# Convolution stage of a gated block: products that span both heads, their sums through PSUM, statistics on ScalarE, three row buffers

## The chip, the cores and the metric

The kernel runs on one core of a Trainium2 chip. The metric is the device time of one execution in microseconds; lower is better. The kernel is written by hand against the engines: TensorE (PE), VectorE (DVE), ScalarE (ACT), GpSimd (POOL) and the DMA-issuing SyncE (SP) each run their own program in order and wait for each other through semaphores.

## The reference

```
x = x + tanh(g_xattn) * xattn(ctx, ctx, layernorm(x), ssm_kernel, D)
x = x + tanh(g_ffn)   * ffn(layernorm(x))

xattn: for batch b, head h (32), rows i, j of the head (8 x 8), length L = 512:
  kv[b,i,j,h,:] = k[b,h,i,:] * v[b,h,j,:]          (k = v = ctx)
  y   = causal convolution of kv with ssm_kernel[h], + D[h] * kv
  out[b,h,j,:] = sum over i of y[b,i,j,h,:] * q[b,h,i,:]
ffn: softmax gate over 16 experts, top 2 routed SwiGLU experts (512 -> 352 -> 512),
  plus two shared ones of the same size, on 2048 rows of 512
```

All of it is float32. Every large matrix is split into a high and a low part, and three products (high by high, high by low, low by high) make one matmul of full precision.

## The kernel before, in words

The first stage has 16 tiles, each of two heads, 8 rows per head and 8 batches: 128 rows of x. A tile's length of 512 is cut into four blocks of 128. Because k = v, only 36 of the 64 products kv of a head are formed (GpSimd, form; ScalarE, square), 288 columns with the batches. conv(t, lb) on TensorE multiplies them with Toeplitz matrices, for each of the two heads into its own PSUM bank (ps_conv[lb % 2] is a pair of banks): 6, 12, 18 and 24 matmuls for blocks 0 to 3. products(t, lb) on VectorE multiplies the result with q (the normalized x, transposed by turn_q and copied by q_copy). A head's 36 pairs give 5 rows of 64 columns that must be added. Three instructions per head do it, one into prod in SBUF and two into ps_rows in PSUM, and a seventh adds the two tiles of 512 into rows. sum_rows(t, lb) on TensorE transposes and adds the four parts of rows and the fifth of prod into a quarter of ps_o with five matmuls against the identity. residual(t) on VectorE then makes x2 out of ps_o, followed by its statistics (bn_stats, bn_aggr), and scale_x2, norm_x2, turn_t, tT_copy and gate make the normalized, transposed x2 and the expert logits.

The order is written out by hand in a function turn(t) for each engine, called for three tiles, then in a loop of two, then for three more (pairs). In tile t:

- TensorE: conv 0, sum_rows(t-1, 3), conv 1, gate(t-2), sum_rows(t, 0), conv 2, sum_rows(t, 1), conv 3, turn_t(t-1), turn_q(t+1), sum_rows(t, 2). conv(t, lb) waits for the products of block lb-2; sum_rows(t, 0) also for x2 of tile t-1, which frees ps_o.
- VectorE: products 0, residual(t-1) with statistics, logits_copy(t-2), products 1, scale_x2(t-1), scale_x(t+1), products 2, products 3.
- ScalarE: split_shared(t), split_kv_hi(t+1), std_x(t+1), std_x2(t-1), square(t+2), norm_x2(t-1), norm_x(t+1), q_copy(t+1), tT_copy(t-1).
- SP (line 467): load ctx(t+3), load x(t+2), store x2(t-1), load xr(t+1), load stage(t+2), store t(t-1), store tT(t-1), load the two Toeplitz parts(t+2). Each store waits for its data, and everything behind it waits too.

The second stage runs the experts: 16 tiles of rows with two shared experts, 47 slots of 128 routed rows. Its schedule is a list of units. Rows of a tile of shared work are loaded by SP (load_rows), rows of a routed tile gathered by GpSimd (gather), into tn[o % 2]; results leave by accumulating indirect DMAs (add_out), each of which waits for the one before it. In GpSimd's program of unit n, gather stands ahead of add_out. The routing itself (maxima, ranks, tables) is computed by VectorE in the first 15 units.

## Time and profile before

| what | value |
|---|---|
| time, median of 3 runs | 743.13 us (741.87 to 744.69) |
| profiled execution | 748.91 us, span 747.1 us |
| TensorE matmuls | 719.4 us busy, 96% of the span |
| TensorE weight loads | 677.7 us, 91% |
| VectorE | 568.9 us, 76% |
| ScalarE | 459.8 us, 62% |
| GpSimd | 369.6 us, 49% |
| mean granted TensorE clock | 0.995 of full speed |
| first stage | first convolution 11.0, last ends 208.1 us |

The matmuls of an engine are pipelined and their ends are modelled: a conv matmul is recorded with 0.30 us while the next one starts 0.13 later, so the distance of the starts says what one costs.

### The profile page before, as it was taken

The page shows a single profiled execution, that of the slowest core. Times are in us where ns is not written, and L with a number is a line of the kernel's source. Part 1 is how long each engine was busy: PE and PEld are TensorE (multiplying, and loading weights), DVE is VectorE, ACT ScalarE, POOL GpSimd, SP SyncE. Part 2 cuts the span into 40 slices and gives each one's busy share as a digit, 9 for nine tenths or more (in the row PEclk, how much of TensorE's full clock was granted, in tenths as well). Part 3 has the DMA queues.
Part 4 walks back from the last instruction along what each step waited for, and adds up shares of the span by engine and source line. Part 5 has one row for each costly group of instructions (what it writes and reads, how often), then busy time and mean ns, then how long its engine had stood idle before and what let it go on. Part 6 is the DMA issues. An engine that isn't in the chain of part 4 may idle for free.

```text
span 747.1 us, 15553 instructions
## 1 busy us (share of the span) xinstructions
PE 719.4 (96%) x4602; PEld 677.7 (91%) x4602; DVE 568.9 (76%) x1111; ACT 459.8 (62%) x659; POOL 369.6 (49%) x190
## 2 busy tenths in 40 slices
PE   3999999999999999999999999999989999999998
PEld 3999999999998999899988999888989999999997
DVE  7899989898955578428889588848977689679942
ACT  7575757566432322136978677747976699678941
POOL 4998888886400065032444444334634445434420
PEclk9999999999999999999999999999999999999999
DMA  7678787776522122463567577767655764332101
GB/s 240 221 231 274 222 265 231 256 235 231 171 100 43 29 43 43 141 184 97 164 201 209 124 234 214 178 174 167 159 159 168 170 194 88 73 67 51 29 16 56
DMA packets 48404, 114.88 MB, mean 154 GB/s; under 512 B 7472, under 2 KB 8624, under 8 KB 48336
## 3 DMA queue, kind: packets, MB, share of 16 engines
q1 hardware_dynamic: 35792, 89.67, 36.9%
q0 software_dynamic: 12544, 24.40, 17.3%
q8 instruction: 31, 0.51, 0.3%
q14 instruction: 37, 0.30, 0.1%
HBM read 157.78 MB, written 29.26 MB: 250 GB/s over the span
## 4 chain that ended last, share of the span: by engine, by line
PE 71%; DVE 11%; DMA 8%; issue 5%; ACT 3%; ACTq 1%; DVEq 0%; SPq 0%; POOLq 0%
PE pair L1304 20%; PE bank L1304 15%; PE pair L1329 12%; PE pair L1235 8%; PE bank L1329 7%; DMA out<-ys,slot_info 5%; PE bank L1186 4%; PE pair L1312 3%; PE bank L1246 2%; DVE prod L830 2%; DVE bank L835 2%; DVE x L801 2%; DVE rows L842 1%; DVE st L781 1%; DVE bank L838 1%
## 5 line engine op out<-in xcount | busy, mean ns | idle before, releaser
L1151 DVE TENSOR_TENSOR w_lo<-raw,w_hi 128x1408 fp32r<-128x1408 f32 x94 | 148.6, 1622 | 49.8 <-ACT w_hi L734 49.7
L1442 POOL DMA_INDIRECT out<-ys,slot_info x47 | 83.0, 1765 | 120.7 <-ACT ys L722 85.5
L1429 POOL DMA_INDIRECT tn<-t_rows,slot_info x47 | 77.2, 1643 | 119.6 <-DVE tT_lo L889 87.5
L734 ACT ACTIVATE w_hi<-raw 128x1408 fp32r x94 | 124.6, 1374 | 3.0 <-issue 2.5
L1235 PE MATMUL pair<-kv_hi,toep_hi 128*128 128x288 f32 x320 | 100.6, 314 | 2.0 <-DMA toep_lo<-kpad_lo 1.7
L1235 PE MATMUL pair<-kv_lo,toep_hi 128*128 128x288 f32 x320 | 95.3, 298 | 0.0
L1235 PE MATMUL pair<-kv_hi,toep_lo 128*128 128x288 f32 x320 | 95.2, 297 | 0.0
L1156 DVE TENSOR_TENSOR w_lo<-raw,w_hi 128x1536 fp32r<-128x1536 f32 x47 | 82.4, 1752 | 6.5 <-ACT w_hi L741 6.5
L1380 POOL TENSOR_TENSOR kv_lo<-kv,kv_hi 128x2304 fp32r<-128x2304 f32 x15 | 77.3, 5155 | 6.1 <-ACT kv_hi L626 6.1
L741 ACT ACTIVATE w_hi<-raw 128x1536 fp32r x47 | 69.2, 1473 | 1.5 <-DMA raw<-in_weights 1.1
L830 DVE TENSOR_TENSOR prod<-pair,q 128x256 f32<-128x256 f32 x128 | 53.5, 418 | 15.5 <-PE pair L1235 10.1
L1160 DVE TENSOR_TENSOR hid<-hid,pair 128x352 f32<-128x352 f32 x44 | 22.7, 517 | 55.4 <-ACT hid L748 55.4
L1235 PEld LDWEIGHTS pair<-kv_hi,toep_hi 128*128 128x128 f32 x320 | 61.0, 191 | 2.8 <-DMA toep_lo<-kpad_lo 2.3
L1235 PEld LDWEIGHTS pair<-kv_lo,toep_hi 128*128 128x128 f32 x320 | 61.2, 191 | 0.0
L1235 PEld LDWEIGHTS pair<-kv_hi,toep_lo 128*128 128x128 f32 x320 | 61.0, 191 | 0.0
L374 POOL TENSOR_TENSOR kv<-cx 128x1536 f32<-128x1536 f32 x15 | 52.6, 3506 | 13.9 <-DMA cx<-in_ctx 13.6
L748 ACT ACTIVATE hid<-pair 128x352 f32<-128x352 f32 x43 | 19.5, 454 | 59.3 <-PE pair L1304 59.2
L1442 POOL DMA_INDIRECT out<-ys,own_row x14 | 26.3, 1876 | 59.8 <-ACT ys L722 51.5
L1304 PE MATMUL pair<-w_hi,tT_hi 128*128 128x352 f32 x192 | 46.3, 322 | 2.6 <-DVE w_lo L1151 2.6
L1304 PE MATMUL pair<-w_hi,tT_lo 128*128 128x352 f32 x192 | 46.1, 321 | 0.0
L748 ACT ACTIVATE hid<-bank 128x352 f32<-128x352 f32 x36 | 16.3, 453 | 48.4 <-PE bank L1304 46.6
L1304 PE MATMUL pair<-w_lo,tT_hi 128*128 128x352 f32 x192 | 46.1, 321 | 0.0
(223 smaller groups left out, 2014.7 us busy)
## 6 DMA issues: line engine op xcount, KB each, us to landing
raw<-in_weights SPq DMA_DIRECT2D x94, 704.0 KB
raw<-in_weights SPq DMA_DIRECT2D x47, 768.0 KB
toep_hi<-kpad_hi SPq DMA_DIRECT2D x15, 512.0 KB, 4.5
toep_lo<-kpad_lo SPq DMA_DIRECT2D x15, 512.0 KB, 6.1
cx<-in_ctx SPq DMA_DIRECT2D x15, 384.0 KB, 6.3
stage<-in_weights SPq DMA_DIRECT2D x16, 272.0 KB, 6.6
xt<-in_x SPq DMA_DIRECT2D x16, 256.0 KB, 6.3
xr<-in_x SPq DMA_DIRECT2D x16, 256.0 KB, 6.5
```

The source lines that it names most:

```text
L374: eng.tensor_tensor(view(z, g0 * k + HB, [[k, g], [HB, 3], [1, HB]]), view(c, g0 * GW, [[GW, g], [0, 3], [1, HB]]), view(c, g0 * GW + BATC ...
L734: act.activation(w_hi[s % 2][:, a:b], raw[:, bass.ds(half + a, b - a)], ACT.Copy).then_inc(hi_ok[n_], 1)
L741: act.activation(w_hi[s % 2][:, W13:WROW], raw[:, bass.ds(half + W13, W2)], ACT.Copy).then_inc(hi_ok[2], 1)
L830: dve.tensor_tensor(view(pp, po, [[P + G, 4], [G, HD], [1, BATCH]]), view(y, 0, [[HB, 4], [BATCH, HD], [1, BATCH]]), view(qq, qo, [[0, 4], ...
L1151: dve.tensor_tensor(w_lo[s % 2][:, a:b], raw[:, bass.ds(half + a, b - a)], w_hi[s % 2][:, a:b].bitcast(F32), ALU.subtract).then_inc(lo_ok[ ...
L1156: dve.tensor_tensor(w_lo[s % 2][:, W13:WROW], raw[:, bass.ds(half + W13, W2)], w_hi[s % 2][:, W13:WROW].bitcast(F32), ALU.subtract).then_i ...
L1235: mm = pe.matmul(ps_conv[lb % 2][:, h * 512:h * 512 + n], w[p][:, k:k + P], z[p][:, o:o + n], start=(mb == 0 and m == 0), stop=(mb == lb a ...
L1304: mm = pe.matmul(dst[:, 0:INTER], a[:, c * P:(c + 1) * P], w[:, f:f + INTER], start=(c == 0 and k == 0), stop=(c == BLOCKS - 1 and k == 2))
L1329: mm = pe.matmul(y_bank(u.o)[:], a[:, c * P:(c + 1) * P], w[:, f0 + c * L:f0 + (c + 1) * L], start=(first and c == 0 and k == 0), stop=(la ...
L1380: pool.tensor_tensor(kv_lo[t.odd][:], kv[t.odd][:], kv_hi[t.odd][:].bitcast(F32), ALU.subtract).then_inc(kvl_ok, 1)
L1429: pool.indirect_dma_start(out=tn[o % 2][:], out_offset=None, in_=t_rows, in_offset=bass.IndirectOffsetOnAxis(ap=slot_info[:, 3 * i:3 * i + ...
L1442: pool.indirect_dma_start(out=out, out_offset=bass.IndirectOffsetOnAxis(ap=rows, axis=0), in_=ys[o % 2][:], in_offset=None, bounds_check=R ...
```

## The change

One products(t, lb) covers both heads with three multiplications: 384 elements into prod (pairs (i, i+1) to (i, i+3) times q of the one member), 128 into prod (pairs (i, i+4), both members), and 512 into ps_rows (pairs (i, i) to (i, i+3) times q of the other member). Three additions of 256 columns follow: in place in ps_rows, into half_sum, and of these two into rows. TensorE is left with three transposes per sum_rows: two of rows and one of prod. The rows of a tile are ordered head first. The statistics of x2 come from two passes with an accumulator on ScalarE, as those of x did already, and std_x(t+2) stands between norm_x and q_copy. In the second stage tn has three buffers, rows are loaded or gathered one tile earlier, and three row tiles are loaded before the last turn of SP. Renamings (o % 2 to o % 3 in the readers of tn, declarations) are left out.

```diff
 PRODROWS = 5
-PROD_STEPS = 6
+PROD_STEPS = 3
+SUMROWS = 2
 EXPERTS, INTER = 16, 352
...
-            u, out = unit(n), []
-            if n == 0:
-                out.append(2)
-            if u and u.last:
-                out.append(u.o + 3)
-            return [o for o in out if o < len(ORDER)]
+            def at(o):
+                return max(last_unit(o - 4), 15 if ORDER[o][0] else 0)
+
+            return [o for o in range(3, len(ORDER)) if at(o) == n]
...
                 routed, j = ORDER[o]
                 if not routed and o not in MID:
-                    wait(sp, tTl_ok, o - 1)
-                    sp.dma_start(tn[o % 2][:], tT_t[j]).then_inc(tn_in[o % 2], 16)
+                    wait(sp, tTl_ok, o - 2)
+                    sp.dma_start(tn[o % 3][:], tT_t[j]).then_inc(tn_in[o % 3], 16)
             sp.wait_ge(kv_ok, 2 * TILES)
             sp.wait_ge(xn_ok, TILES)
-            for p in (0, 1):
-                sp.wait_ge(tT_out[p], 16)
-            load_rows(0)
-            load_rows(1)
+            sp.wait_ge(tT_out[0], 32)
+            sp.wait_ge(tT_out[1], 16)
+            for o in range(3):
+                load_rows(o)
             turn(At(TILES - 1))
             for which in ("x2", "t", "tT"):
...
             act.activation(small[:, 3:4], small[:, 0:1], ACT.Sqrt)
+            def stats(src, mv, ok, t):
+
+                p = t.odd
+                act.activation(spent[:], src[p][:], ACT.Copy, scale=-1.0 / L, accum_out=mv[p][:, 0:1]).then_inc(ok, 1)
+                wait(act, ok, t * 2 + 1)
+                act.activation(spent[:], src[p][:], ACT.Square, bias=mv[p][:, 0:1],
+                               accum_out=mv[p][:, 1:2]).then_inc(ok, 1)
+                wait(act, ok, (t + 1) * 2)
+
             def std_x(t):
-
-                p = t.odd
-                wait(act, x_in[p], (t.half() + 1) * 16)
+                wait(act, x_in[t.odd], (t.half() + 1) * 16)
                 wait(act, rstd1, (t - 1) * 2)
-                act.activation(spent[:], xt[p][:], ACT.Copy, scale=-1.0 / L, accum_out=mv1[p][:, 0:1]).then_inc(stat1, 1)
-                wait(act, stat1, t * 2 + 1)
-                act.activation(spent[:], xt[p][:], ACT.Square, bias=mv1[p][:, 0:1],
-                               accum_out=mv1[p][:, 1:2]).then_inc(stat1, 1)
-                wait(act, stat1, (t + 1) * 2)
-                act.activation(sd1[p][:, 0:1], mv1[p][:, 1:2], ACT.Sqrt, bias=small[:, 0:1],
+                stats(xt, mv1, stat1, t)
+                act.activation(sd1[t.odd][:, 0:1], mv1[t.odd][:, 1:2], ACT.Sqrt, bias=small[:, 0:1],
                                scale=1.0 / L).then_inc(std1, 1)
             def std_x2(t):
-                wait(act, stat2, (t + 1) * 2)
-                act.activation(sd2[t.odd][:, 0:1], mv2[t.odd][:, 1:2], ACT.Sqrt, bias=small[:, 0:1]).then_inc(std2, 1)
+                wait(act, x2_ok, t + 1)
+                wait(act, rstd2, (t - 1) * 2)
+                stats(x2, mv2, stat2, t)
+                act.activation(sd2[t.odd][:, 0:1], mv2[t.odd][:, 1:2], ACT.Sqrt, bias=small[:, 0:1],
+                               scale=1.0 / L).then_inc(std2, 1)
             def norm_x(t):
...
                 wait(act, prod_ok, (t - 1) * 4 * PROD_STEPS)
                 wait(act, q_turned, t + 1)
-                src = ps_q[:].rearrange("p (l c) -> p l c", l=BLOCKS)
-                dst = q[p][:].rearrange("p (l c) -> p l c", l=BLOCKS)
-                act.activation(dst[:, :, 0:P], src, ACT.Copy).then_inc(q_ok, 1)
-                act.activation(dst[:, :, P:], src[:, :, 0:GROUPS * EXT - P], ACT.Copy).then_inc(q_ok, 1)
+                act.activation(view(q[p][:], 0, [[2 * GW, BLOCKS], [GW, 2], [1, HB]]),
+                               view(ps_q, 0, [[P, BLOCKS], [HB, 2], [1, HB]]), ACT.Copy).then_inc(q_ok, 1)
+                act.activation(view(q[p][:], HB, [[2 * GW, BLOCKS], [GW, 2], [1, HB // 2]]),
+                               view(ps_q, 0, [[P, BLOCKS], [HB, 2], [1, HB // 2]]), ACT.Copy).then_inc(q_ok, 1)
             def tT_copy(t):
...
                 if first:
                     std_x(t + 1)
+                if first:
                     split_kv_hi(t + 1)
                 split_shared(t)
                 if not first and not last:
                     split_kv_hi(t + 1)
-                    std_x(t + 1)
                 if not first:
                     std_x2(t - 1)
...
                 if not last:
                     norm_x(t + 1)
+                if not t.within(TILES - 2, TILES):
+                    std_x(t + 2)
+                if not last:
                     q_copy(t + 1)
                 if not first:
...
                 dve.scalar_tensor_tensor(x2[p][:], ps_o[:], small[:, 1:2], xr[p][:],
                                          ALU.mult, ALU.add).then_inc(x2_ok, 1)
-                wait(dve, x2_ok, t + 1)
-                stats(x2, st2, mv2, stat2, t)
             def scale_x2(t):
                 p = t.odd
                 wait(dve, std2, t + 1)
                 dve.reciprocal(sd2[p][:, 1:2], sd2[p][:, 0:1]).then_inc(rstd2, 1)
                 wait(dve, rstd2, t * 2 + 1)
-                dve.tensor_scalar(mv2[p][:, 2:3], mv2[p][:, 0:1], sd2[p][:, 1:2], -1.0,
-                                  ALU.mult, ALU.mult).then_inc(rstd2, 1)
+                dve.tensor_scalar(mv2[p][:, 2:3], mv2[p][:, 0:1], sd2[p][:, 1:2], None,
+                                  ALU.mult).then_inc(rstd2, 1)
             def products(t, lb):
                 par = lb % 2
-                G, HB = GROUPS, HD * BATCH
-                for h in range(2):
-                    y = ps_conv[par][:, h * 512:h * 512 + 512]
-                    qo = lb * GROUPS * EXT + h * BATCH
-                    po = h * BATCH
-                    qq, pp = q[t.odd][:], prod[par][:]
-                    if h == 0:
-                        wait(dve, summed, t * 4 + lb - 1)
-                        if lb == 0:
-                            wait(dve, q_ok, (t + 1) * 2)
-                    wait(dve, conv_ok, t * 8 + 2 * lb + h + 1)
-                    dve.tensor_tensor(view(pp, po, [[P + G, 4], [G, HD], [1, BATCH]]),
-                                      view(y, 0, [[HB, 4], [BATCH, HD], [1, BATCH]]),
-                                      view(qq, qo, [[0, 4], [G, HD], [1, BATCH]]), ALU.mult).then_inc(prod_ok, 1)
-                    if h == 0:
-                        wait(dve, rows_ok, t * 4 + lb)
-                    dve.tensor_tensor(view(ps_rows, po, [[P, 3], [G, HD], [1, BATCH]]),
-                                      view(y, HB, [[HB, 3], [BATCH, HD], [1, BATCH]]),
-                                      view(qq, qo + G, [[G, 3], [G, HD], [1, BATCH]]), ALU.mult).then_inc(prod_ok, 1)
-                    dve.tensor_tensor(view(ps_rows, po + 3 * P, [[4 * G, 2], [G, 4], [1, BATCH]]),
-                                      view(y, 4 * HB, [[0, 2], [BATCH, 4], [1, BATCH]]),
-                                      view(qq, qo + 4 * G, [[4 * G, 2], [G, 4], [1, BATCH]]), ALU.mult).then_inc(prod_ok, 1)
+                y, z, w = ps_conv[par][:], q[t.odd][:], prod[par][:]
+                qo, n = lb * 2 * GW, 4 * HB
+                wait(dve, summed, t * 4 + lb - 1)
+                if lb == 0:
+                    wait(dve, q_ok, (t + 1) * 2)
+                wait(dve, conv_ok, t * 8 + 2 * lb + 2)
+                dve.tensor_tensor(view(w, BATCH, [[n, 2], [HB + BATCH, 3], [1, HB]]),
+                                  view(y, HB, [[512, 2], [HB, 3], [1, HB]]),
+                                  view(z, qo, [[GW, 2], [0, 3], [1, HB]]), ALU.mult).then_inc(prod_ok, 1)
+                dve.tensor_tensor(view(w, 2 * n, [[HB, 2], [HB // 2, 2], [1, HB // 2]]),
+                                  view(y, 4 * HB, [[512, 2], [0, 2], [1, HB // 2]]),
+                                  view(z, qo + HB // 2, [[GW, 2], [HB // 2, 2], [1, HB // 2]]),
+                                  ALU.mult).then_inc(prod_ok, 1)
+                wait(dve, rows_ok, t * 4 + lb)
+                dve.tensor_tensor(view(ps_rows, 0, [[HB, 2], [P, 4], [1, HB]]),
+                                  view(y, 0, [[512, 2], [HB, 4], [1, HB]]),
+                                  view(z, qo, [[GW, 2], [BATCH, 4], [1, HB]]), ALU.mult).then_inc(prod_ok, 1)
                 wait(dve, prod_ok, (t * 4 + lb + 1) * PROD_STEPS)
-                dve.tensor_tensor(rows[par][:], ps_rows, prod[par][:, 0:L], ALU.add).then_inc(rows_ok, 1)
+                m = SUMROWS * P
+                dve.tensor_tensor(ps_rows[:, m:], ps_rows[:, m:], view(w, 2 * HB, [[HB, 2], [n, 2], [1, HB]]),
+                                  ALU.add).then_inc(half_ok, 1)
+                dve.tensor_tensor(half_sum[:], ps_rows[:, 0:m], view(w, 0, [[HB, 2], [n, 2], [1, HB]]),
+                                  ALU.add).then_inc(half_ok, 1)
+                wait(dve, half_ok, (t * 4 + lb + 1) * 2)
+                dve.tensor_tensor(rows[par][:], ps_rows[:, m:], half_sum[:], ALU.add).then_inc(rows_ok, 1)
             def first_kv_lo(a, b, ok):
...
                     wait(pe, x2_ok, t)
                 wait(pe, rows_ok, t * 4 + lb + 1)
-                for r in range(PRODROWS):
-                    part = (rows if r < BLOCKS else prod)[lb % 2]
-                    mm = pe.matmul(ps_o[:, lb * P:(lb + 1) * P], part[:, r * P:(r + 1) * P], ident[:],
-                                   is_transpose=True, start=(r == 0), stop=(r == PRODROWS - 1))
+                last = prod[lb % 2][:, 8 * HB:]
+                for r in range(SUMROWS + 1):
+                    part = rows[lb % 2][:, r * P:(r + 1) * P] if r < SUMROWS else last
+                    mm = pe.matmul(ps_o[:, lb * P:(lb + 1) * P], part, ident[:],
+                                   is_transpose=True, start=(r == 0), stop=(r == SUMROWS))
                 mm.then_inc(summed, 1)
...
                     pool.wait_ge(r_done, 1)
-                wait(pool, tTl_ok, o - 1)
-                pool.indirect_dma_start(out=tn[o % 2][:], out_offset=None, in_=t_rows,
+                wait(pool, tTl_ok, o - 2)
+                pool.indirect_dma_start(out=tn[o % 3][:], out_offset=None, in_=t_rows,
                                         in_offset=bass.IndirectOffsetOnAxis(ap=slot_info[:, 3 * i:3 * i + 1], axis=0),
-                                        bounds_check=ROWS - 1, oob_is_err=False).then_inc(row_in[o % 2], 16)
+                                        bounds_check=ROWS - 1, oob_is_err=False).then_inc(row_in[o % 3], 16)
...
-    x_rows = x.reshape(BATCH, TILES, 2, HD, L).transpose(1, 3, 2, 0, 4).reshape(ROWS, L)
+    x_rows = x.reshape(BATCH, TILES, 2, HD, L).transpose(1, 2, 3, 0, 4).reshape(ROWS, L)
```

## Rows read from the trace of the kernel before

**Rows 1.** Busy time by stretch, 13 tiles of the first stage: from, to, length, busy.
```profile
38.61:197.94 159.33, 157.58 (x1250) 154.52 (x1250) 144.45 (x481) 101.81 (x182) 134.11 (x50) 1.00 0.75 240
```
**Rows 2.** Instructions in order of time, VectorE, one tile: start, length, idle before.
```profile
97.91 0.42 DVE L830 TENSOR_TENSOR prod<-pair,q 128x256 f32<-128x256 f32 x1 [0.48 <-PE pair L1235]
...
99.86 0.42 DVE L830 TENSOR_TENSOR prod<-pair,q 128x256 f32<-128x256 f32 x1 [0.39 <-ACT q L612]
...
100.46 0.22 DVE L838 TENSOR_TENSOR bank<-pair,q 128x64 f32<-128x64 f32 x1
100.59 0.42 DVE L830 TENSOR_TENSOR prod<-pair,q 128x256 f32<-128x256 f32 x1
...
101.19 0.22 DVE L838 TENSOR_TENSOR bank<-pair,q 128x64 f32<-128x64 f32 x1
101.45 0.69 DVE L842 TENSOR_TENSOR rows<-bank,prod 128x512 f32<-128x512 f32 x1
102.05 0.74 DVE L801 SCALAR_TENSOR_TENSOR x<-bank,small,xr 128x512 f32<-128x512 f32 x1
...
103.91 0.42 DVE L830 TENSOR_TENSOR prod<-pair,q 128x256 f32<-128x256 f32 x1
...
106.74 0.41 DVE L830 TENSOR_TENSOR prod<-pair,q 128x256 f32<-128x256 f32 x1
```
**Rows 3.** The same view, TensorE, around the same tile.
```profile
97.58 0.30 PE L1235 MATMUL pair<-kv_hi,toep_lo 128*128 128x288 f32 x1
...
98.15 0.60 PE L1186 MATMUL bank<-ident,xn 128*128 128x128 f32 x4
...
103.92 0.29 PE L1235 MATMUL pair<-kv_hi,toep_hi 128*128 128x288 f32 x1
...
105.51 0.29 PE L1235 MATMUL pair<-kv_hi,toep_hi 128*128 128x288 f32 x1
...
106.25 0.66 PE L1246 MATMUL bank<-ident,rows 128*128 128x128 f32 x4 [0.18 <-DVE rows L842]
...
106.77 0.38 PE L1235 MATMUL pair<-kv_hi,toep_hi 128*128 128x288 f32 x1
```
**Rows 4.** The same view, ScalarE and SP's queue, the same tile.
```profile
98.85 0.60 ACT L611 ACTIVATE q<-bank 128x512 f32<-128x512 f32 x1 [3.03 <-PE bank L1186]
...
99.60 0.60 ACT L618 ACTIVATE tT<-bank 128x512 f32<-128x512 f32 x1
...
102.65 0.64 ACT L577 ACTIVATE spent<-xt 128x512 f32<-128x512 f32 x1
...
104.46 0.28 ACT L587 ACTIVATE sd<-mv,small 128x1 f32<-128x1 f32 x1
...
100.23 0.35 SPq L465 DMA_DIRECT2D tT_rows<-tT  x1
...
103.09 0.35 SPq L434 DMA_DIRECT2D xt<-in_x  x1
```
**Rows 5.** DMA issues, from 36 to 204 us and to 48 us: count, KB, landing.
```profile
xt<-in_x SPq DMA_DIRECT2D x12, 256.0 KB, 6.2
...
xt<-in_x SPq DMA_DIRECT2D x1, 256.0 KB, 8.0
```
**Rows 6.** Hand-over: order of time (TensorE, ScalarE), then the chain of waits.
```profile
228.52 0.59 PE L1304 MATMUL pair<-shared_hi,tT_hi 128*128 128x352 f32 x2 [1.81 <-DVE hid L1160]
...
222.72 0.63 ACT L707 ACTIVATE tT_hi<-tn 128x512 fp32r<-128x512 f32 x1 [2.30 <-DMA tn<-tT_rows]
...
228.52 5.68 PE pair L1304 x24
...
236.85 3.81 PE pair L1304 x24
```
**Rows 7.** Second stage: TensorE in order of time, then waits in total.
```profile
546.58 0.99 PE L1186 MATMUL bank<-ident,tn 128*128 128x128 f32 x4 [1.89 <-DMA tn<-t_rows,slot_info]
...
ACT ys L722 <- DMA out<-ys,slot_info: 34.4, 14, 6.4
```

More of the change, by code:

```diff
@@ L208, in program @@
         x2 = sb2("x2", [P, L], F32, one)
-        st2 = sb2("st2_", [P, 6], F32, one)
         mv1, mv2 = sb2("mv1_", [P, 3], F32, one), sb2("mv2_", [P, 3], F32, one)
@@ L217, in program @@
         prod = sb2("prod", [P, PRODROWS * P], F32, one)
-        rows = sb2("rows", [P, L], F32, one)
+        rows = sb2("rows", [P, SUMROWS * P], F32, one)
+        half_sum = sb("half_sum", [P, SUMROWS * P], F32, one)
         spent = sb("spent", [P, L], F32, one)
@@ L223, in program @@
         one.close()
-        tn = sb2("tn", [P, L])
+        tn = [sb(f"tn{n}", [P, L]) for n in range(3)]
         tn_mid = sb("tn_mid", [P, L])
@@ L290, in program @@
         r_fields, r_info, r_done = sem("r_fields"), sem("r_info"), sem("r_done")
-        tn_in, row_in, tn_mid_in = sem2("tn_in"), sem2("row_in"), sem("tn_mid_in")
+        tn_in, row_in = [sem(f"tn_in{n}") for n in range(3)], [sem(f"row_in{n}") for n in range(3)]
+        tn_mid_in = sem("tn_mid_in")
         tile_turned, tTh_ok, tTl_ok = sem("tile_turned"), sem("tTh_ok"), sem("tTl_ok")
@@ L355, in tn_count @@
         def tn_count(o):
-            return 16 * sum(ORDER[k][0] == ORDER[o][0] and k not in MID for k in range(o % 2, o + 1, 2))
+            return 16 * sum(ORDER[k][0] == ORDER[o][0] and k not in MID for k in range(o % 3, o + 1, 3))
         def last_unit(o):
@@ L776, in _ @@
             dve.tensor_tensor(krow_lo[:], krow[:], krow_hi[:].bitcast(F32), ALU.subtract).then_inc(krowl_ok, 1)
-            def stats(src, st, mv, ok, t):
-                p = t.odd
-                dve.bn_stats(st[p][:], src[p][:]).then_inc(ok, 1)
-                wait(dve, ok, t * 2 + 1)
-                dve.tensor_copy(hop[:, 1:2], hop[:, 0:1])
-                dve.bn_aggr(mv[p][:, 0:2], st[p][:]).then_inc(ok, 1)
             def scale_x(t):
@@ L1275, in turn_tile @@
             def turn_tile(o):
[L1276 removed]
+                pe.wait_ge(row_in[o % 3], tn_count(o))
                 wait(pe, tTl_ok, o)
[L1278 removed]
+                turn_rows(tn[o % 3], ps_t, tile_turned)
             def parts(hi, lo, whi, wlo):
```

15 lines of the change are left out of this document (7 added, 8 removed).

## The prediction

> **What bounds the kernel now.** I read the busy time by stretch first, then the instructions of one tile in order of time on each engine, then the DMA issues, and last the chain of waits after the first stage. In 159.3 us the first stage does 13 tiles, so a tile takes 12.26 us [rows 1]. TensorE is busy for 99% of them and VectorE for 91%, which looks like a TensorE that only needs less work. The order of time says otherwise: both engines stand in one loop and wait for each other once or twice per tile.
>
> The loop of today can be followed in the tile whose first product starts at 99.86 [rows 2]. VectorE does products of block 0 (to 102.05, so 2.19 us for a block), the residual, the statistics of x2, a logits copy and block 1, whose rows release TensorE's sum_rows at 106.25, after it sat idle [rows 3]. Then come 24 matmuls of block 3, 8 transposes, q_copy, and the next tile's first product, which had to wait for q_copy [rows 2, 4]. Check of the loop: 106.25 - 99.86 = 6.39; 0.60 for five transposes and the first conv's late start; 24 x 0.1325 = 3.18 (twelve conv matmuls take 105.51 - 103.92 = 1.59); turn_t 0.44; from turn_q's start to q_copy 0.70 and to the product 1.01 more [rows 3, 4]. Sum 12.32, against 12.26 measured. So I trust sums of this kind to 0.1 us.
>
> **The change, first stage.** Call the start of block 0's products zero.
>
> *Cost of products.* The old block has seven instructions over 1536 elements, the new one six over 1792 (384, 128, 512 multiplied; 256 + 256 + 256 added). A successor that waits for nothing starts 0.09 us before the record of its predecessor ends (100.46, 0.22 long, next at 100.59); one that waits for its result starts 0.04 after it (101.19, 0.22 long, next at 101.45) [rows 2]. An element costs (0.69 - 0.42)/256 = 1.05 ns. So: 384 elements 0.42 + 0.13 - 0.09 = 0.46; 128 elements 0.28 - 0.09 = 0.20; 512 elements with a wait behind it 0.69 + 0.04 = 0.73; add 0.33; add with a wait 0.46; add 0.33. Sum 2.51, so 0.32 more than 2.19. The pattern (runs of 64 in place of runs of 8) I price at nothing: the old ones already run at one element per 1.05 ns. No row shows an instruction that reads and writes the same PSUM bank, as the first add does. Bounds: 0 (it goes like the other mixes of PSUM and SBUF) to doubling, 0.27 per block; I take 0, the nearest rows, 0.42 for 256 elements out of PSUM.
>
> *The Trainium skill* ("VectorE: DVE Perf Modes", section "The DRAIN you can't avoid") says that the pipeline empties after every operation anyway and a semaphore wait costs nothing extra. The trace does not agree: the same 64-element product is followed after 0.13 us without a wait and after 0.26 with one [rows 2].
>
> *The new loop.* Block 0 ends at 2.51; the residual takes 0.74 and its result is seen 0.05 later: 3.30. Here TensorE waits in sum_rows(t, 0), because it may not write ps_o before x2 is out. Five transposes after a wait took 106.77 - 106.25 = 0.52 [rows 3]; three take 0.30, the first conv matmul's late start 0.08: 3.68. 18 conv matmuls: 2.39, 6.07. Three transposes: 0.33, 6.40. 24 conv matmuls: 3.18, 9.58. The products of block 3 now need both heads. Before, they did head 0 while TensorE computed head 1, and only head 1 was left at 97.91, 0.20 behind the end of the last conv matmul's slot (97.58 + 0.13) [rows 2, 3]. Now all of block 3 comes after it: start 9.78, end 12.29, and there the next tile's first product stands. Tile: **12.29 us**, 0.03 more than now. The 8 transposes less (0.88 us) and the statistics gone from VectorE (103.91 - 102.05 less 0.65 for the residual and some 0.12 for the logits copy, 1.09 us) are real, but they are given back: twice 0.32 for longer blocks, and the overlap lost at block 3, whose bare part grows from 1.46 us (0.73 for head 1, 0.13, 0.60) to 2.51. Fourteen tiles: +0.4.
>
> *What lies beside this loop.* q_copy: 9.58 + 0.44 + 0.70 + 1.01 = 11.73, 0.56 before it is needed [rows 4]. VectorE's own sum: 4 x 2.51 + 0.65 + 0.12 + 0.64 of scales (106.74 - 103.91 - 2.19) = 11.5. The statistics of x2 on ScalarE: the same pair of passes and the root for x take 104.46 - 102.65 = 1.81 [rows 4], from 3.3 to 5.2, and scale_x2 comes at 5.8; the cover is 0.6. ScalarE waited 3.03 us per tile before q_copy, and std_x(t + 2), moved there, takes 1.81 of it. But it must have x(t + 2), and that closes a second loop: tT_copy, SP's store of it, two toeplitz loads, ctx, the x load (issued 103.09 - 100.23 = 2.86 later), landing after 6.2 [rows 4, 5], statistics 1.81, 0.75 to tT_copy's start (99.60 - 98.85), 0.60 for it: 12.2 us and two hops. That ties with 12.29. In steady state I take nothing; one early tile has its x landing after 8.0 [rows 5], which costs (8.0 - 6.2 less slack of about 1.0) +0.8 once. The first tile, where block 3's products also lie bare, +0.3.
>
> **The change, hand-over and second stage.** The last block 3 ends 1.05 later behind its convolution and tT_lo(0) stands behind it; TensorE has its last gate and sums to do in the meantime, so I take +0.7 (bounds 0 and 1.05). Against this, row tile 2 of the expert stage is loaded before the last turn's stores, no longer behind them. ScalarE waited 2.30 us for it, and behind it stand tT_lo(2), the routing's first operations and the hidden rows of unit 2, for which TensorE sat idle 1.81 us. Its next 24 matmuls took 5.68 us where 3.81 is normal [rows 6]: after the idle the granted clock fell to its lower level (1.2 GHz) for part of them. The chain gets 2.3 us earlier while TensorE gets 0.7 later, so I take both: -1.8 and -1.9. Bounds: 0 to -4.2.
>
> Gathers of routed rows: fills_at moves each by one tile and the wait from o - 1 to o - 2, so at a given place of POOL's queue the same tT_lo is awaited; the add-outs behind it are not freed. What goes is TensorE's wait for a late gather, in the longest case 1.89 us and transposes of 0.99 instead of 0.60 [rows 7]. The larger waits here, ScalarE for earlier add-outs, 34.4 us in 14 times [rows 7], stay, and would swallow part of what an early gather gives. I take -1.2, bounds 0 to -6. SP's earlier row loads wait for results that are old by then: 0. More bytes move nowhere.
>
> **Sum.** First stage +0.4 + 0.8 + 0.3 = +1.5; hand-over +0.7 - 1.8 - 1.9 = -3.0; gathers -1.2; together **-2.7 us**. The profiled execution took 748.9 (span 747.1, 1.8 around it), so it would take 746.2; the runs' median, 743.1, lies 5.8 below the profiled one, and I move it by the same: **740.5 us**. I read "same" as within 0.5%, 3.7 us: 739.4 to 746.8.
>
> **Rivals.**
> - *The load of x decides (slower).* The second loop takes over once x lands more than about 0.1 to 0.3 us later than 6.2. For it: the tie, and landings of up to 8.0 [rows 5]. Against it: the transfers of one burst share a queue, so a later issue is likely to land sooner. At 0.5 us per tile: 14 x 0.5 = +7, 747.5. It decides from a tile of 12.55 us upward. Chance 0.20.
> - *The in-place add in one PSUM bank runs at half speed (slower).* Two blocks of the loop: 14 x 2 x 0.27 = +7.6, 748. Chance 0.08.
> - *Waits inside the products cost nothing (faster).* Each block would be 0.26 shorter, the loop 0.52, to 11.77; then the x loop (12.1) decides: -0.2 x 14 = -2.7, 737.8. For it stands only that TensorE and VectorE have less work each. Chance 0.12. This is also what the skill's rule above would make of it.
> - *The third buffer smooths the expert stage (faster).* If the stalls behind add-outs shrink too, with gathers landed early: 5 us more than I took, 735.5. Against it: they follow add-outs. Chance 0.15.
> - *Hand-over bound by another thing*, such as POOL's constants for the routing: nothing gained there but nothing lost, 744. Chance 0.06.
>
> Forecast 0.39; its own range 737.5 to 744. Faster by over 0.5%: the two fast rivals and 0.12 of the forecast's own, 0.39. Slower: the two slow ones less a little, 0.26. Within: 0.35. For eight in ten I take 735.5 to 748.5.
>
> **What would show it.** Products of 384, 128 and 512 elements of about 0.56, 0.28 and 0.69 us, adds of 0.42; 2.5 us per block; block 3's first product idle behind PE by about 0.8 us and the next tile's first product waiting for nothing; TensorE idle about 0.8 us before sum_rows(t - 1, 3) and 0.3 before sum_rows(t, 0). If that product waits for q_copy and ScalarE's first pass over x waits for its DMA, the second loop decides. If tiles take under 12.0, my cost of a block or of the bare block 3 is wrong. At the hand-over: no fall of the clock near 230 us. If it stays, the routing chain has another start than tile 2.

## The result: 6 us slower, and the profile after

| | median | range | runs |
|---|---|---|---|
| before | 743.13 us | 739.15 to 748.21 | 19 |
| changed | 749.71 us | 744.32 to 753.81 | 19 |

The ratio is 1.0082, 95% interval 1.0061 to 1.0104, so 6.1 us slower; on a second chip it was 1.0054 (1.0027 to 1.0082), 4.0 us. 740.5 was forecast, and the time lies outside the range. The profiled execution of the changed kernel took 747.88 us (span 746.0), that of the kernel before 748.91. So between the two executions whose traces are read here the changed kernel is 1.0 us faster, while over all runs it is 6.1 us slower: the traces show where single stages grew or shrank, and the runs decide the whole.

Busy time in the stretch of [rows 1], changed kernel (from, to, length; TensorE, its weight loads, VectorE, ScalarE, GpSimd, each with its count; granted clock, DMA share, GB/s):
```profile
38.61:197.94 159.33, 144.10 (x1116) 139.92 (x1115) 143.73 (x385) 122.08 (x228) 133.64 (x50) 1.00 0.75 238
```
TensorE fell from 99% to 90% busy and VectorE stayed at 90%: work was taken off, and the stage became longer. Where it went is seen in one tile of VectorE, in order of time (start, length, idle before), which answers to [rows 2]:
```profile
102.97 0.56 DVE L825 TENSOR_TENSOR prod<-pair,q 128x384 f32<-128x384 f32 x1 [0.26 <-issue]
103.44 0.28 DVE L828 TENSOR_TENSOR prod<-pair,q 128x128 f32<-128x128 f32 x1
103.64 0.69 DVE L833 TENSOR_TENSOR bank<-pair,q 128x512 f32<-128x512 f32 x1
104.36 0.43 DVE L838 TENSOR_TENSOR bank<-bank,prod 128x256 f32<-128x256 f32 x1
104.70 0.41 DVE L840 TENSOR_TENSOR half_sum<-bank,prod 128x256 f32<-128x256 f32 x1
105.15 0.43 DVE L843 TENSOR_TENSOR rows<-bank,half_sum 128x256 f32<-128x256 f32 x1
105.49 0.74 DVE L803 SCALAR_TENSOR_TENSOR x<-bank,small,xr 128x512 f32<-128x512 f32 x1
...
112.91 0.56 DVE L825 TENSOR_TENSOR prod<-pair,q 128x384 f32<-128x384 f32 x1 [0.93 <-PE pair L1236]
...
115.44 0.55 DVE L825 TENSOR_TENSOR prod<-pair,q 128x384 f32<-128x384 f32 x1
```
The same tile on TensorE (with the idle rows that answer to [rows 3]) and then on ScalarE [rows 4]:
```profile
102.76 0.44 PE L1248 MATMUL bank<-ident,rows 128*128 128x128 f32 x2 [0.71 <-DVE rows L843]
...
106.36 0.43 PE L1248 MATMUL bank<-ident,rows 128*128 128x128 f32 x2 [0.66 <-DVE x L803]
...
109.13 0.38 PE L1248 MATMUL bank<-ident,rows 128*128 128x128 f32 x2
...
112.64 0.60 PE L1187 MATMUL bank<-ident,t 128*128 128x128 f32 x4
```
```profile
111.41 0.63 ACT L576 ACTIVATE spent<-xt 128x512 f32<-128x512 f32 x1 [0.64 <-DMA xt<-in_x]
...
113.77 0.60 ACT L616 ACTIVATE q<-bank 128x512 f32<-128x512 f32 x1 [0.47 <-PE bank L1187]
```
The reader is to see the loop that was drawn: products of block 0, residual, sum of rows on TensorE, blocks 2 and 3 of the convolution, block 3's products bare behind them, and the next tile's product without a wait. From 102.97 to 115.44 it takes 12.47 us. At each of the four boundaries of VectorE's loop (two tiles per pass) VectorE idles 0.26 to 0.33 us more, put down to "issue" (the first line above is one of them), and the tile takes 12.74 to 12.82.

Starts of turn_q (L1187, the TensorE row that reads xn) in the two kernels, read from the same view:

| | tile 1 | tile 15 | a tile, mean of 14 | last conv matmul | expert stage starts | unit 3 | table's matmuls |
|---|---|---|---|---|---|---|---|
| before | 24.33 | 196.26 | 12.28 | 207.84 | 210.74 | 228.52 | 305.95 |
| changed | 24.83 | 200.71 | 12.56 | 212.53 | 216.28 | 232.41 | 308.23 |
| difference | +0.5 | +4.45 | +0.28 | +4.7 | +5.5 | +3.9 | +2.3 |

Unit 3 is the one whose up-projection (24 matmuls) TensorE waited 1.81 us for in the kernel before [rows 6]; the table's matmuls are the 32 that build the routing table.

The hand-over, chain of waits from 215 to 245 us, changed kernel, and the row in it of TensorE [rows 6]:
```profile
225.05 0.81 PE bank L1208 x8
225.98 0.08 issue
226.06 0.24 POOL io L1407
...
227.22 0.53 POOL upper L1418
227.74 0.06 issue
227.80 0.16 POOL own_row L1420
...
229.52 2.41 DVE mi L920 x17
231.93 0.43 DVE hid L1161
232.41 4.15 PE pair L1306 x24
```
```profile
232.41 0.59 PE L1306 MATMUL pair<-shared_hi,tT_hi 128*128 128x352 f32 x2 [0.17 <-DVE hid L1161]
```
The 1.81 us of idle and the 5.68 us are gone. What holds the routing's start is now the last gate (L1208) and GpSimd's constants behind it.

### The profile page after: what moved, and what is told of

The parts are those of the page before. It is cut to its first block, busy times and chain, and to the rows that moved or that the text cites. A ratio compares the mean times of both kernels' runs of the same rounds, so it can differ in the third digit from the quotient of the medians.

```text
span 746.0 us, 15248 instructions
## 1 busy us (share of the span) xinstructions
PE 706.5 (95%) x4474; PEld 664.1 (89%) x4474; DVE 571.2 (77%) x999; ACT 486.4 (65%) x723; POOL 366.6 (49%) x190
## 4 chain that ended last, share of the span: by engine, by line
PE 66%; DVE 12%; DMA 11%; issue 5%; ACT 2%; POOL 1%; DVEq 1%; ACTq 1%; SPq 0%; POOLq 0%
PE pair L1306 18%; PE pair L1236 13%; PE bank L1306 13%; PE pair L1331 11%; DMA out<-ys,slot_info 9%; PE bank L1331 6%; PE pair L1314 3%; DVE bank L833 2%; PE bank L1248 2%; PE bank L1187 2%; DVE bank L838 2%; DVE x L803 2%; DVE half_sum L840 1%; DVE prod L825 1%; DVE prod L828 1%
## 5 line engine op out<-in xcount | busy, mean ns | idle before, releaser
L1444 POOL DMA_INDIRECT out<-ys,slot_info x47 | 80.9, 1721 | 122.1 <-ACT ys L732 89.6
L825 DVE TENSOR_TENSOR prod<-pair,q 128x384 f32<-128x384 f32 x64 | 35.3, 552 | 16.6 <-PE pair L1236 15.4
```

The source lines that it names most:

```text
L825: dve.tensor_tensor(view(w, BATCH, [[n, 2], [HB + BATCH, 3], [1, HB]]), view(y, HB, [[512, 2], [HB, 3], [1, HB]]), view(z, qo, [[GW, 2], [ ...
L1444: pool.indirect_dma_start(out=out, out_offset=bass.IndirectOffsetOnAxis(ap=rows, axis=0), in_=ys[o % 2][:], in_offset=None, bounds_check=R ...
```

## The experiments

Each kernel was timed beside the kernel before on its chip. "Parts" are parts of the change alone, put on the kernel before.

**1. The third buffer alone.** Only the row buffers and semaphores by o % 3 and what goes with them:
```
+        tn = [sb(f"tn{n}", [P, L]) for n in range(3)]
-                    wait(sp, tTl_ok, o - 1)
+                    wait(sp, tTl_ok, o - 2)
```


> The kernel before with the third row buffer alone (tn[o % 3], gathers and row loads one tile earlier); the first stage is the one of before. All theories: last convolution ends at 208.1 us as before; the expert stage's up-projection of unit 3 starts 1.8 us earlier and without the slow stretch behind it, so unit 4 starts 3.5 us earlier than at 236.9. Theory A (the first stage alone makes the changed kernel slower, the third buffer only helps): total 3.5 us below before. Theory B (the third buffer costs some 4 us in the expert stage, as the medians suggest: both profiles stand 2.3 us apart at 350 us, the medians 6.6): total as before, within 1 us. Theory C (the new order of rows in a tile costs it): like A, 3.5 below, since this kernel keeps the old order.

Measured: 740.68 us, ratio 0.9961 (0.9938 to 0.9984), faster by 2.9; 3.5 was expected. In its trace, first in order of time and then in the chain of waits, the hand-over is that of the forecast:
```profile
227.18 0.59 PE L1303 MATMUL pair<-shared_hi,tT_hi 128*128 128x352 f32 x2 [0.30 <-DVE hid L1159]
```
```profile
227.18 4.14 PE pair L1303 x24
233.98 3.81 PE pair L1303 x24
```
Unit 4 begins at 233.98 and not at 236.85: 2.9 us, as large as the gain of the runs. 1.34 of it is the idle and 1.5 the fall of the clock (4.14 us for the 24 matmuls against 5.68). The runs of before hold that fall only as far as it is usual there; of the four kernels with two row buffers three have it in their profile (before and 2 with 5.68, 4 with 5.67), and 3 has not (4.14). On the first stage of before the third buffer does no harm in total.

**2. The first stage alone** (the changed kernel with two row buffers, the edit above undone).

> The changed kernel with two row buffers as before, so the first-stage change alone, with the new order of rows. All theories: tiles of 12.5 us on average, last convolution ends at 212.8, and the wait at the hand-over is back (unit 4 starts near 242). Theory A: 5.3 us above before, and the changed kernel would then be 3.5 us faster than this one, which its own median (6.6 above before) contradicts. Theory B: 5.3 above before, the changed kernel 1 us slower than this one. Theory C: 9 to 10 us above before.

Measured: 751.42 us, ratio 1.0094 (1.0064 to 1.0123), slower by 7.0. Its tiles are those of the changed kernel, 12.47 and 12.75 to 12.81, and unit 4 starts at 242.9: the wait at the hand-over is back. 1.0094 x 0.9961 = 1.0055: the two parts add up to the change within the intervals.

**3. The statistics alone**, on the kernel before: statistics of x2 on ScalarE and std_x moved; old products.
```
-                std_x(t + 2)          # before norm_x2
+                    std_x(t + 2)      # behind norm_x(t + 1)
+            def std_x2(t):
+                stats(x2, mv2, stat2, t)
```


> The kernel before with only the statistics of x2 on ScalarE (and std_x(t+2) between norm_x and q_copy). The loop of before loses 1.1 us on VectorE (11.2), so TensorE's own sum decides, 60 x 0.1325 + 28 x 0.11 + 0.9 = 11.9, with hops 12.0 a tile, if the x load's loop (12.1 to 12.3) allows it: 14 x -0.15 to -0.25, total 2 to 3.5 us below before. Rival: the x load's loop holds the tile at 12.26 or above: no gain, or a loss of up to 2 us.

Measured: 743.38 us, ratio 0.9995 (0.9976 to 1.0014). Its steady tiles take 12.1 us, which would gain about 2 us; but two tiles early in the stage took 12.95 and 15.45, where the first pass over x waited up to 4.0 us for its load. The waits from 36 to 66 us (engine, line, what for, total, times, longest):
```profile
ACT spent L574 <- DMA xt<-in_x: 9.5, 3, 4.0
DVE prod L828 <- PE pair L1233: 4.2, 7, 0.8
DVE prod L828 <- ACT q L617: 3.9, 2, 2.4
```
Here the second loop of the forecast is real: the load of x decides.

**4. The products alone**: new products, sums and three transposes; statistics still on VectorE.

> The kernel before with only the new products and sums (and the new order of rows), statistics of x2 still on VectorE. My loop over the residual and the bare block 3 gives 12.47 as in the changed kernel; VectorE's own sum is now 4 x 2.53 + 0.65 + 0.12 + 0.63 + 0.97 of statistics = 12.5, with the loop's branch in every second tile 12.7: 14 x 0.45, total 5 to 8 us above before. Rival (block 3's lost overlap is not on the path, the slow part lies elsewhere): tile of 12.26, total as before.

Measured: 762.46 us, ratio 1.0265 (1.023 to 1.0301), slower by 18 to 20. Its tile is 13.3 and 13.7 us, more than any theory had. VectorE, in order of time:
```profile
107.94 0.56 DVE L828 TENSOR_TENSOR prod<-pair,q 128x384 f32<-128x384 f32 x1 [0.28 <-issue]
...
110.47 0.74 DVE L804 SCALAR_TENSOR_TENSOR x<-bank,small,xr 128x512 f32<-128x512 f32 x1
111.24 0.69 DVE L784 BATCH_NORM_STATS2 st<-x 128x6 f32<-128x512 f32 x1
...
112.32 0.56 DVE L828 TENSOR_TENSOR prod<-pair,q 128x384 f32<-128x384 f32 x1
...
118.82 0.56 DVE L828 TENSOR_TENSOR prod<-pair,q 128x384 f32<-128x384 f32 x1 [0.73 <-PE pair L1239]
```
The loop passes over block 1 here: statistics lie between residual and block 1, whose rows TensorE needs before block 3 (112.32 + 2.6 = 114.9, then 0.4 of transposes, 3.18 of block 3, hop), and block 3's products stand bare behind that. So the products cost 18 us, and moving the statistics, worth nothing by itself, gives 11 of them back (762.46 against 751.42 in 2). Parts that lie in one loop do not add.

**5. The changed kernel again**, beside 6 to 8.

> The changed kernel itself, timed again beside the three that follow. At the first routing table's matmuls it stood 2.3 us behind the kernel before in the two profiles (308.2 against 305.9 us), while the medians differ by 6.1. Theory A (the difference is made in the first stage, and the profile of before is itself an unlucky one, 5.8 us above its median): the table at 308 to 309 us again and a time 5 to 7 us above before, about 749. Rival B (part of the 6.1 is made in the expert stage by the other row buffers or by the transfers that fall otherwise): the profile again at 308 us, but from there to the end some 3 us more than in the kernel with the third buffer alone (which needed 435.9 us from there to its end); A has 435 to 437 for that stretch.

Measured: 748.57 us, ratio 1.0054 (1.0027 to 1.0082); the profile (745.97) has the table's matmuls at 307.78 and 436.4 us from there to the end. This profile is as A has it, but it does not refute rival B. The same expert stage took 437.8 us in the first profile of the changed kernel, and 440.1 and 439.9 in those of 8 and 9. Over all the kernels' profiles that stretch is 434.4 (experiment 4) to 441.2 (the kernel before): the mean of the four with two row buffers is 437.6, that of the ten with three 438.9. B stays open, as a difference of 1 to 3 us that single profiles don't tell apart.

**6. TensorE's turn in another order**, on the changed kernel. Nothing is computed otherwise; conv gets a list of heads.
```
                 conv(t, 0)
+                conv(t, 1)
                 sum_rows(t - 1, 3)
-                conv(t, 1)
                 gate(t - 2)
+                conv(t, 2, (0,))
                 sum_rows(t, 0)
-                conv(t, 2)
+                conv(t, 2, (1,))
+                conv(t, 3, (0,))
                 sum_rows(t, 1)
-                conv(t, 3)
+                conv(t, 3, (1,))
```


> The changed kernel with TensorE's turn in another order: both blocks 0 and 1 before the sum of the last rows, and the sums of blocks 0 and 1 each put between the two heads of the convolution two blocks on. Theory A (a tile of the first stage is a closed chain VectorE block 3, VectorE block 0 and residual, TensorE sum of rows, convolutions 2 and 3, VectorE block 3; 12.47 us and 12.8 across the loop's branch): 0.66 us that TensorE waited for x2 and 0.7 for the rows before it are filled with convolution, so the tile falls to 11.7 to 12.1, 14 tiles give 7 to 12 us, and the time is 738 to 743. Rival C (the loop of the x load, xn done, load issued, x landed, statistics, xn, decides as soon as the other is shortened; 12.1 us a tile in the kernel with only the statistics moved): tile 12.1 to 12.3 with q_copy late and block 0 waiting for it, time 742 to 746. Rival D (VectorE's work itself binds, 4 x 2.52 + 0.8 + 0.5): tile 11.4 to 11.6 with no wait on VectorE, time 733 to 738.

Measured: 742.78 us, ratio 0.9968 (0.9942 to 0.9995), 5.8 under the changed kernel. The steady tiles are 11.8 to 12.1, as A and nearly C allow, and the idle before block 0's products and before the pass over x says C:
```profile
102.03 0.56 DVE L825 TENSOR_TENSOR prod<-pair,q 128x384 f32<-128x384 f32 x1 [0.57 <-ACT q L618]
...
114.11 0.56 DVE L825 TENSOR_TENSOR prod<-pair,q 128x384 f32<-128x384 f32 x1 [0.54 <-ACT q L618]
```
```profile
111.33 0.63 ACT L576 ACTIVATE spent<-xt 128x512 f32<-128x512 f32 x1 [1.50 <-DMA xt<-in_x]
```

**7. Block 3's products by head**, on the changed kernel.
```
-                wait(dve, conv_ok, t * 8 + 2 * lb + 2)
+                each = lb == 3
+                for h, k in ((0, 1), (1, 1)) if each else ((0, 2),):
+                    wait(dve, conv_ok, t * 8 + 2 * lb + h + k)
                     (the three products over k heads from head h)
```


> The changed kernel with block 3's three products made for each head apart, the first head's as soon as its convolution is done. Theory A (what decides is that VectorE now starts block 3 only when both heads are convolved, and does nothing in the 0.93 us before): products of head 0 (0.28 + 0.14 + 0.35 = 0.77 us) go into that wait, three instructions' fixed cost of about 0.1 each comes back, so block 3 ends about 0.6 us earlier and the tile is 11.9 to 12.0; 14 tiles give 8 us and the time is 740 to 743. Rival C (the x load's loop takes over at about 12.1 to 12.3): 742 to 746, with block 0 waiting for q_copy. Rival E (block 3's wait is not what decides, but the whole of VectorE's work): the fixed costs are added, tile 12.6 to 12.9 and time 749 to 754.

Measured: 741.89 us, ratio 0.9962 (0.9932 to 0.9993), 6.7 under the changed kernel; its tiles are 12.2 at VectorE's four loop boundaries, 11.9 to 12.0 elsewhere, and once 12.25; three early ones are 12.1 to 12.6. So theory A has the time and, but for the boundaries, the tile. The first head's products run in what was idle, and the second's start at the old hop behind the convolution. From 40 to 180 us VectorE idles for 2.0 us, against 10.3 in the changed kernel: what decides here is VectorE's own work with the branch of its loop. The x load only ties, though ScalarE waits 1.1 to 1.7 us for it in most tiles: the last line below is at a loop boundary, and its 0.26 us, put down to q_copy, is as long as the branch in the changed kernel; a wait for q_copy alone (0.28) is seen in one steady tile, at 112.92.
```profile
97.49 0.35 DVE L829 TENSOR_TENSOR prod<-pair,q 128x192 f32<-128x192 f32 x1
...
98.34 0.36 DVE L829 TENSOR_TENSOR prod<-pair,q 128x192 f32<-128x192 f32 x1
...
100.67 0.56 DVE L829 TENSOR_TENSOR prod<-pair,q 128x384 f32<-128x384 f32 x1 [0.26 <-ACT q L619]
```

**8. VectorE without its loop**, on the changed kernel.
```
-            pairs(dve, turn)
+            for t in range(TILES):
+                turn(At(t))
```


> The changed kernel with VectorE's instructions of the first stage written out tile by tile, with no loop (the other engines keep theirs). In the trace of the changed kernel every second tile takes 12.8 instead of 12.47 us, and block 0's first product there follows an idle 0.3 us put down to issue. Theory A (the branch of VectorE's loop, formerly behind the wait for q_copy, stands bare in the chain): all tiles 12.45 to 12.5, 5 branches of 0.3 us away, time 1.5 to 2 us less than the changed kernel, about 747.5. Rival F (the alternate tiles are another engine's branch, TensorE's or ScalarE's, or the even tiles' loads): they stay 12.8, and the time is that of the changed kernel. Rival G (more code for VectorE brings waits for its instructions): tiles 12.6 to 13, time above 750.

Measured: 748.66 us, ratio 1.0058 (1.0032 to 1.0083). The 12.8 us tiles at the boundaries are gone: VectorE's tiles are 12.39 to 12.47, but for two of 12.72 and 12.81 where q_copy came 0.23 and 0.26 late. So theory A has the place right. The expert stage starts 1.2 us earlier (214.76 against 215.97), of which 0.7 lies already before tile 1 (turn_q at 23.78 against 24.50). The time shows nothing of it: 1 us is below what these medians tell apart, and in this profile the granted clock in the hand-over (the figure behind the last count, 0.94; 1.00 in experiment 5) took back as much. The stretch from 205 to 232 us in 8 and in 5:
```profile
205.00:232.00 27.00, 25.89 (x165) 24.75 (x164) 16.35 (x84) 11.42 (x24) 1.74 (x8) 0.94 0.28 96
```
```profile
205.00:232.00 27.00, 25.48 (x175) 24.06 (x173) 17.93 (x88) 11.46 (x24) 1.74 (x8) 1.00 0.31 110
```
F and G fall by the tiles.

**9. The load of x early**, on the changed kernel.
```
-                if ahead:
+                if first:
                     wait(sp, xn_ok, t + 1)
                     load(t + 2, "x")
...
                 if not first:
                     store(t - 1, "t")
+                if not t.within(TILES - 3, TILES):
+                    wait(sp, xn_ok, t + 2)
+                    load(t + 3, "x")
                 if not first:
                     store(t - 1, "tT")
```


> The changed kernel with one thing moved: SyncE issues the load of x(t + 3) right behind the store of t(t - 1), where its buffer is already free, instead of behind the store of tT, the Toeplitz and the context loads of the next turn. Theory A (in the changed kernel the closed chain through block 3 decides and the x load's loop only ties with it): ScalarE's wait for x (0.6 to 0.8 us a tile) goes, its wait for TensorE before q_copy grows by as much, tiles stay 12.47 and 12.8, time 748 to 749. Rival C (the x load's loop is what made the changed kernel slow): tiles fall to 12.1 to 12.3, time 742 to 745.

Measured: 748.37 us, ratio 1.0053 (1.0025 to 1.0081): nothing. The load lands after 3.2 us and not 6.2, ScalarE starts its pass at once and waits for TensorE afterwards, and the tiles stay 12.47 and 12.8. This rival of the forecast is refuted for the changed kernel.
```profile
111.00 0.62 ACT L580 ACTIVATE spent<-xt 128x512 f32<-128x512 f32 x1
```
```profile
113.23 0.56 DVE L829 TENSOR_TENSOR prod<-pair,q 128x384 f32<-128x384 f32 x1 [0.92 <-PE pair L1240]
```

**10. New order and early load together** (edits 6 and 9).

> The reordered TensorE turn (12.1 us a tile, 742.8) together with the early load of x. Theory A: there the x load's loop decides (ScalarE 1.5 us behind the load, block 0's first product 0.57 behind q_copy), so with it gone the tile falls by about 0.5 to VectorE's own sum, 4 x 2.52 + 0.74 + 0.08 + 0.64 = 11.5, plus 0.16 for its loop's branch, 11.7; 14 tiles give 5 to 6 us and the two tiles of 13.3 and 13.9 early in the stage, where x landed late by up to 2.9 us, give 1 to 2 more: 735 to 737. Rival H (TensorE's sum, about 11.3, with its wait for x2, now binds): tile 11.9 to 12.0, 740 to 741. Rival I (the two early tiles are not the x load's): 737 to 738.

Measured: 733.82 us, ratio 0.9867 (0.9835 to 0.9898). The same move of one load that gave nothing in 9 gives 1.0% here (0.9968 to 0.9867, or 742.78 to 733.82 us), more than expected, since the slow early tiles vanish too. Tiles are 11.44, and 11.8 across the branch. From 40 to 180 us VectorE has 1.1 us of waits in all. The stretch of [rows 1]:
```profile
38.61:197.94 159.33, 156.31 (x1219) 152.70 (x1217) 153.48 (x414) 123.58 (x235) 134.70 (x51) 1.00 0.77 247
```

**11. The same without VectorE's loop** (edits 6, 8 and 9).

> The same with VectorE's first stage written out without a loop. Theory A (VectorE without a wait decides there, so a branch of 0.3 us every second tile is bare): all tiles 11.5 to 11.6, time 1 to 2 us less than the kernel above, 734 to 736. Rival: the branch is hidden by a remaining wait, no difference.

Measured: 732.51 us, ratio 0.9827 (0.9796 to 0.9859): the fastest kernel here, 16 to 17 us under the changed one and 11 to 13 under the one before. All tiles but the first are 11.44, and VectorE has no wait at all from 40 to 180 us, so the branch was bare in 10. For the step from 10 to 11, 1.3 us, the two intervals overlap; the tiles show it, the time alone does not.

**12. All but the products**, on the kernel before: third buffer, statistics on ScalarE, early x; old products, five transposes.

> The kernel before with the third row buffer, the statistics of x2 on ScalarE and the early load of x, but with its own products and five transposes per sum of rows. Theory A: its TensorE is busy for 99% of the tile, so the tile cannot fall below TensorE's work, about 12.1; the kernel with only the statistics moved was there already but lost 3 us early to a late x, which goes, and the buffer gives 3 us: 736 to 739. Rival J (the busy share of TensorE hides waits, and the tile falls to 11.8 or less once both loops are relieved): 732 to 735. Rival K (the early x collides with the stores and context loads, which land later): 741 to 744.

Measured: 737.73 us, ratio 0.9897 (0.9863 to 0.9931). The time is theory A's, the tile of 11.91 lies between A's 12.1 and rival J's 11.8, and TensorE is full:
```profile
38.61:197.94 159.33, 159.33 (x1289) 159.33 (x1288) 137.71 (x457) 124.09 (x235) 135.72 (x51) 1.00 0.77 246
```
Only against this kernel do three transposes in place of five pay: 11.44 against 11.91 us a tile, once the loop of the new products has been opened. This kernel keeps the old order of TensorE's turn; with TensorE busy all the time there is no idle for another order to fill, but that was not run. It also says what the changes are worth apart from the products: 5.8 of the 11 us (743.53 to 737.73) come without them.

## Why the prediction was wrong, step by step

- **Cost of a block, 2.51.** Right: 102.97 to 105.49 is 2.52. The in-place add takes 0.43, so the rival with half speed falls. The waits inside are not free: a 256-element add is followed 0.34 after its start without a wait (104.36 to 104.70) and 0.45 with one (104.70 to 105.15). The Trainium skill ("VectorE: DVE Perf Modes", "The DRAIN you can't avoid") says of a chain of copies that the semaphore costs nothing extra; this trace differs again, by 0.11, and the measurement decides.
- **The loop, 12.29.** The mechanism was right, and the term was too small: this is the step that failed by most. Residual until sum_rows 0.87 (105.49 to 106.36) where 0.79 was put, TensorE's part 6.55 (to 112.91) where 6.48 was, block 3 2.53. That makes 12.47. The hops came from rows where the waiting engine had stood idle for a shorter time: 0.05 (TensorE idle 0.18) against 0.13 (idle 0.66) for the residual, 0.20 (VectorE idle 0.48) against 0.27 (idle 0.93) behind the convolution. That the hop grows with the idle is read from these four rows and was not tested.
- **VectorE's loop branch, not in the sum at all.** In the kernel before, block 0's products waited 0.39 us for q_copy [rows 2] and the branch lay beneath. In the changed kernel the forecast said itself that this product waits for nothing, and did not ask what that wait had covered. Mean over 14 tiles: 12.56, so 14 x 0.28 = +3.9 us where +0.4 stood; 14 x 0.18 = 2.5 of the 3.5 missing are nearly all hops, and the four bare branches of 0.26 to 0.33 are the other 1.
- **First tile and late x, +1.1.** Measured +0.5, and that is no effect of the change: with the first stage of before, experiment 1 has tile 1 at 25.03. By tile 15 this evens out (196.26 and 196.44 in before and 1, 200.38 to 201.09 in the changed kernel, 2, 5 and 9). No tile was lengthened by a late x in the changed kernel.
- **Last block, +0.7.** From turn_q of tile 15 to the expert stage +1.1 (5.54 - 4.45), just over its bound.
- **Hand-over, idle, -1.8.** Right: from the start of the expert stage to unit 3 17.78 became 16.13, -1.65, though it ends at GpSimd's constants, which was a rival's mechanism.
- **Hand-over, clock, -1.9.** Between the two profiles the fall at this place is gone, as forecast, but that is worth 1.5 and not 1.9 (5.68 to 4.15; without a fall the 24 matmuls take 4.14 there, as in 3, and not 3.81). It is wrong for the time, because the falls did not become fewer. None of the ten profiles with three row buffers has it at unit 3. But nine of them have one between 455 and 515 us, and no profile with two buffers has one there. In the changed kernel this one follows TensorE's wait for VectorE's w_lo (the low part of a routed expert's weights). In experiment 5, the same kernel, a wait as long is followed by none. Each block has the first matmul behind the wait and then the 4 us from there (the clock is the third figure from the end):
```profile
507.79 0.62 PE L1306 MATMUL pair<-w_hi,tT_hi 128*128 128x352 f32 x2 [2.68 <-DVE w_lo L1152]
...
508.00:512.00 4.00, 4.00 (x17) 4.00 (x17) 4.00 (x4) 2.62 (x2) 2.75 (x2) 0.57 0.70 152
```
```profile
506.17 0.56 PE L1306 MATMUL pair<-w_hi,tT_hi 128*128 128x352 f32 x2 [2.85 <-DVE w_lo L1152]
...
506.00:510.00 4.00, 3.83 (x24) 3.86 (x25) 4.00 (x5) 3.01 (x3) 2.87 (x2) 1.00 0.81 164
```
  The profile of before holds two falls, at the hand-over and at 547 us, and a mean clock of 0.995; that of the changed kernel holds one and 0.998. Of the 74 runs of before beside the experiments two had 0.995 and the others 0.997 to 1.0, with medians of 743.5 to 744.5. The changed kernel had 0.993 or 0.995 in 6 of 19 and 4 of 12 runs. The median clock of both is 0.998, so I count nothing of the 1.9 as gained. Whether the same cause moved the fall is not shown.
- **Gathers, -1.2.** Not borne out. The 3.2 us that TensorE waited for gathers behind the table [rows 7] belong to one execution: the other kernels with two row buffers waited 1.7, 0.2 and 0 us (2, 3, 4). With three buffers that wait is gone, but the longest wait for w_lo grew from 1.6 to 2.0 us with two buffers to 2.1 to 3.8 with three, and the stretch from the table to the end got no shorter (437.6 and 438.9 us on average, experiment 5). That the third buffer makes the longer wait is not shown.
- **The move to the median, -5.8.** The terms for the clock and the gathers were read from an execution that lay above all 19 runs of before, and then taken off their median. For the gathers the three other profiles with two buffers show that most executions hold less of this loss; for the clock the median holds one fall in place of two (0.998 against 0.995).

Sum of what is shown: 3.9 + 0.5 + 1.1 - 1.65 = +3.9 us, with nothing for clock and gathers, against 6.1 (4.5 to 7.7) and 4.0 (2.0 to 6.1) measured. It explains the second chip's figure; about 2 us of the first one's stay open, of which a lower clock in more of its runs (mean 751.8 in the six at 0.993 or 0.995, 748.0 in the other thirteen, so 6/19 x 3.8 = 1.2 us on the mean) and a longer expert stage (rival B of experiment 5) may be parts; neither was tested. Of the 8.8 us between the forecast change (-2.7) and the measured one (+6.1) the loop is 3.5, the clock 1.9, the gathers 1.2, about 2.2 are open, and the small terms cancel. The loop alone, put right, would have given 744, about the time of before: the other two were needed to turn the forecast round.

The x load as the deciding rival got 0.20 and would have given a like time, by a mechanism that 9 refutes. It ties, as forecast, and decides once the first loop is opened by the new order (6), though not when it is opened at block 3 (7).

## What to carry to other kernels

Where two engines wait for each other, neither engine's busy share falls due when work is taken from it: write the loop with its hops, and take hops from rows where the waiting engine had stood idle as long as the change will make it. Before a forecast lets a wait vanish, ask what lay under it: here a loop branch on the same engine. The same edit can be worth 0 or some 8 us depending on which loop is closed (9 and 10), so test it again once the first loop is open. And a loss seen in one profiled execution is worth only its frequency among the runs: here the waits for gathers were large in one execution of four, and the fall of the clock came back at another wait.

## What the runs showed of the hardware

- A taken loop branch on VectorE costs 0.26 to 0.33 us of idle, and it vanishes when the tiles are written out (8, 11). The Trainium skill ("Runtime: NRT & Kernel Launch", "Instruction fetch mechanics") warns that a taken branch stalls the fetch where its target lies outside the current window of two pages; the trace shows an idle at that place, and neither its cause nor where the target lies.
- The 256 KB load of x issued right behind 1.4 MB of Toeplitz and context loads lands after 6.2 us (median of 12), and issued behind one store of 256 KB after 3.2 (9).
- An add that reads and writes one PSUM bank takes 0.43 us for 256 elements, like those that read PSUM and write to other memory, 0.41 to 0.43.
- The fall of TensorE's granted clock to half comes behind a wait of TensorE, but not behind each: behind 2.68 us in the changed kernel and not behind 2.85 in experiment 5; behind 1.81 us at the hand-over in before and not behind 1.70 in experiment 3. It costs 1.5 us on 24 matmuls (5.68 against 4.14).
